# Two feed-forward passes over eight experts: the lead between the two products, and which engine rectifies which tile

## The chip, the cores and the metric

The kernel runs on one NeuronCore of one Trainium2 chip. The metric is the device time of one execution in microseconds (us). TensorE (PE) multiplies and transposes, ScalarE (ACT) and VectorE (DVE) read PSUM and write SBUF, GpSimd (POOL) issues the indirect DMAs, SyncE (SP) the direct ones. Each engine runs its own queue in order and waits on semaphores.

## The reference, cut to what matters

```python
def _L0_ffn_ref(tgt, Wr, br, W1, b1, W2, b2, gamma, beta):
    logits = jnp.einsum('bsd,ed->bse', tgt, Wr) + br
    top_v, top_i = jax.lax.top_k(logits, 2)
    ...
    h = jax.nn.relu(jnp.einsum('bsd,efd->bsef', tgt, W1) + b1)
    o = jnp.einsum('bsef,edf->bsed', h, W2) + b2
    tgt2 = jnp.einsum('bsed,bse->bsd', o, router_w)
    return _layer_norm(tgt + tgt2, gamma, beta)
x = x + 0.5 * _L0_ffn_ref(_layernorm(x), ...)
x = x + _L0_attn_ref(_layernorm(x), ...)
x = x + 0.5 * _L0_ffn_ref(_layernorm(x), ...)
```

There are 4 batches of 1024 rows, D = 128, F = 512, 8 experts, two experts to a row, all in float32. The attention is a difference of two softmaxes; the change does not touch it.

## The kernel before

**Stages.** Setup and first routing take up to about 51 us, the first expert pass 51 to 210 us, attention over four batches 210 to 450 us, the second expert pass 450 to 622 us, and the merge of the last two batches the rest.

**An expert pass** works on tiles of 128 routed rows, all of one expert. There are two groups (two batches each) of GSLOTS = 39 tiles, so SLOTS = 78 tiles to a pass; T counts tiles over both passes. For tile T, PE transposes the gathered rows into bank 0 (`turn_x`, L1059). ACT copies the result to SBUF (`copy_xT`, L692) and copies the expert's first weight, 128x512, to a staging buffer (`stage_w1`, L698). PE makes the first product in four blocks of 128 hidden units (`first`, L1066), which the profile shows as 8 records. ACT rectifies blocks 0 and 1 (`relu_first`, L705), DVE blocks 2 and 3 (`relu_rest`, L1579). PE accumulates the second product over the four blocks (`second`, L1076, again 8 records), and DVE adds the bias b2 and stores the tile in a ring of 16 (`add_b2`, L1587). The first product of a tile lies in two PSUM banks, two blocks in each, and two tiles alternate in banks 2 to 5. The y tiles alternate in banks 6 and 1. `xT`, `w1s` and `hT` have two buffers each, cut from `scratch` by `lent`.

**The order is written out by hand.** Each engine has its own `step(p, s)`. On PE, step s is `turn_x(s+2)`, `first(s+1)`, `second(s)`. On ACT it is `copy_xT(s+2)`, `stage_w1(s+2)`, `relu_first(s+1)`. On DVE it is `add_b2(s-1)`, `relu_rest(s+1)`. The loops run from s = -2. `turn_x(T)` waits for `xT_sb >= T`, that is, until ACT has copied tile T-1 out of bank 0. `second(T)` also waits for `add_b2(T-2)`. `expert_offset` loads the register with the place of tile s+2's expert on each engine.

**Side work sits between steps.** In pass one DVE carries the routing of the second group (s = 0 to 18) and, from s = 49, the merge of batch 0 in pieces (`MERGING`, `first_merge`); its 13th piece, at s = 61, is `batch_stats` (L1332). In pass two DVE does `last_route` in steps 0 to 3, whose fourth piece is again `batch_stats`. ACT makes rows in two halves of four normalisations (L644) at s = 5 and 6 of pass two and rescales sums in the same manner at s = 66, 67, 75 and 76.

**POOL** works one list in order. In pass one it gathers the rows of each tile (`gather_x`, L486, one indirect DMA), five up front and later as far as the transposes allow. After tile 55 it mixes these with gathers of results (L507); `rstd(BATCHES)`, which waits for the statistics of s = 61, stands just ahead of `gather_x(68)`, and tiles 68 to 77 follow. In pass two the rows are loaded by SP (`load`, L383), and POOL writes every finished tile to `results` (`send`, L518). Its list there is: three scatters (L494), `rstd(n)` (waits for the fourth piece of `last_route`), three scatters, then 78 sends; one scatter follows each of the first ten, and two follow each of sends 16 to 23. `rstd` stands again after sends 63 and 72. SP loads tile T into its ring slot only when send T-16 has landed, and tile 39, the first of the second group, only when all scatters have landed (`group_ready(1)`).

The change touches `hT_at`, `hT_of`, `staged`, `xT_of`, `copy_xT`, `stage_w1`, `relu_first`, `relu_rest`, `first`, `second`, the three `step` functions and the loop starts.

Of the kernel before, what the change touches and what calls it, by code (L numbers as in the profile page):

```python
# [14 lines left out]
P = 128  # L15
# [15 lines left out]
def macaron_kernel(nc, x_in, w_q12, w_k12, w_v, lq1, lk1, lq2, lk2, Wr, br, W1, b1, W2, b2, gamma, beta, out):  # L31
    BATCHES, S, D = x_in.shape
    E, F, _ = W1.shape
# [26 lines left out]
    with ctx:  # L60
# [91 lines left out]
        xt, xT, w1s, hT, ys = lent(RING * ROW), lent(2 * P), lent(2 * F), lent(2 * F), lent(RING * D)  # L152
        assert at[0] <= ATT
# [5 lines left out]
        def lent_z(n):  # L159
# [9 lines left out]
        assert at[0] <= ATT  # L169
# [14 lines left out]
         xT_ps, xT_sb, hT_ps, hT_sb, y_ps, y_sb,  # L184
# [7 lines left out]
            "hT_ps", "hT_sb", "y_ps", "y_sb", "z_used", "xn_ready",  # L192
# [12 lines left out]
        hT_first = sem("hT_first")  # L205
# [29 lines left out]
        def xT_of(T):  # L235

            return xT[:, T % 2 * P:(T % 2 + 1) * P]

        def staged(T, c, n=1):

            return w1s[:, T % 2 * F + c * P:T % 2 * F + (c + n) * P]

        def hT_at(T, c):

            return bank(2 + 2 * (T % 2) + 2 * c // FC, c % (FC // 2) * P, (c % (FC // 2) + 1) * P)

        def hT_of(T, c):

            return hT[:, (T % 2 * FC + c) * P:(T % 2 * FC + c + 1) * P]
# [47 lines left out]
        Y_BEHIND, Y_NEAR = 12, 7  # L297
        BETA_AT = 18
# [322 lines left out]
        def _(act):  # L621
# [66 lines left out]
            def copy_xT(T):  # L688
                act.wait_ge(xT_ps, T + 1)
                if T >= 2:  # L690
                    act.wait_ge(hT_ps, 2 * T - 2)
                act.activation(xT_of(T), bank(0, 0, P), ACT.Copy).then_inc(xT_sb, 1)  # L692

            def stage_w1(T, at):

                if T >= 2:
                    act.wait_ge(hT_ps, 2 * T - 2)
                act.activation(staged(T, 0, FC), blocks[:, bass.ds(at, F)], ACT.Copy).then_inc(w1_sb, 1)  # L698

            def relu_first(T, at):  # L700
                act.wait_ge(hT_ps, 2 * T + 1)
                if T >= 2:
# [3 lines left out]
                ins.then_inc(hT_first, 1)  # L706
# [186 lines left out]
            for s in range(-2, SLOTS):  # L893
# [3 lines left out]
                if s == GSLOTS - 3:  # L897
# [14 lines left out]
            for s in range(-2, SLOTS):  # L912
# [10 lines left out]
                if s == GSLOTS - 3:  # L923
# [27 lines left out]
        def _(pe):  # L951
# [109 lines left out]
            def first(T):  # L1061
# [180 lines left out]
            for s in range(-2, SLOTS):  # L1242
                if s == GSLOTS - 2:
# [13 lines left out]
            for s in range(-2, SLOTS):  # L1257
                if s in (TURN_AT, TURN_AT + 1):
                    turn_rows(a, s - TURN_AT)
                if s == GSLOTS - 2:  # L1260
# [34 lines left out]
        def _(dve):  # L1295
# [278 lines left out]
            def relu_rest(T, at):  # L1574
                dve.wait_ge(hT_ps, 2 * T + 2)
                if T >= 2:
                    dve.wait_ge(y_ps, T - 1)
                for c in range(FC // 2, FC):
                    ins = dve.tensor_scalar(hT_of(T, c), hT_at(T, c), blocks[:, B1_AT + c:][:, bass.ds(at, 1)], 0.0, ALU.add, ALU.max)  # L1579
                ins.then_inc(hT_sb, 1)  # L1580
# [10 lines left out]
            def step(p, s):  # L1591
# [349 lines left out]
            for s in range(-2, SLOTS + 1):  # L1941
# [33 lines left out]
            for s in range(-2, SLOTS + 1):  # L1975
# [59 lines left out]
```

## Time and profile before

| what | value |
|---|---|
| device time, median of 3 runs | 656.39 us (655.84 to 657.74) |
| the profiled execution: time, span | 657.03 us, 655.3 us |
| PE busy | 586.6 us, 90% of the span |
| DVE, ACT, POOL busy | 452.0, 441.4, 388.8 us |
| first product, L1066, 1248 records | 171.2 us busy, mean 281 ns |
| second product, L1076, 1248 records | 167.1 us busy, mean 277 ns |
| mean granted TensorE clock | 0.954 |

A matmul record shows 275 ns but the next one starts about 0.11 us later: they overlap, and the pace is read from starts. The timeline merges equal instructions in a row ("x8") and gives the idle time of the engine before them with what ended it in square brackets. A granted clock of 1.00 is 2.4 GHz, 0.50 is 1.2 GHz.

### The profile page before, as it was taken

How to read it: one execution, taken by the hardware profiler on the slowest of the kernel's cores; microseconds unless marked ns; L12 is line 12 of the kernel's file. 1: busy time of each engine (PE TensorE's matmuls, PEld its weight loads, DVE VectorE, ACT ScalarE, POOL GpSimd, SP SyncE). 2: the span in 40 equal slices, each digit the busy share in tenths (PEclk: the TensorE clock that was granted, in tenths of full speed). 3: DMA queues.
4: the chain of work that ended last, by engine and by line, in shares of the span. 5: the costliest groups of instructions: out<-in, count | busy, mean ns of one | idle time of the engine just before them, and what ended most of it. 6: DMA issues, size and time to landing. Idle time of an engine off the chain costs nothing.

```text
span 655.3 us, 16513 instructions
## 1 busy us (share of the span) xinstructions
PE 586.6 (90%) x4362; PEld 538.8 (82%) x4362; DVE 452.0 (69%) x1421; ACT 441.4 (67%) x1146; POOL 388.8 (59%) x481
## 2 busy tenths in 40 slices
PE   5987999999998888899898999798999959999945
PEld 5877999999998677787796888687999959998911
DVE  4775788446685989699689868956567534477635
ACT  4755666676667586768885975775876636877724
POOL 3006565657577785587424575784577777655623
PEclk9587999999999999899999999997999998999968
DMA  8902223223234110000000000112233323621051
GB/s 249 313 23 58 78 74 75 79 77 88 74 72 84 44 30 9 18 24 26 2 1 2 12 30 25 42 44 57 65 75 88 104 66 84 210 79 40 29 192 65
DMA packets 41881, 45.96 MB, mean 70 GB/s; under 512 B 8726, under 2 KB 32706, under 8 KB 41536
## 3 DMA queue, kind: packets, MB, share of 16 engines
q1 hardware_dynamic: 32496, 27.13, 14.2%
q0 software_dynamic: 9088, 17.75, 9.8%
q8 instruction: 39, 0.64, 0.4%
q14 instruction: 50, 0.41, 0.2%
q10 hardware_dynamic: 208, 0.02, 0.0%
HBM read 25.95 MB, written 19.83 MB: 70 GB/s over the span
## 4 chain that ended last, share of the span: by engine, by line
PE 47%; DVE 21%; POOL 10%; issue 9%; ACT 8%; DMA 3%; DVEq 0%; ACTq 0%; SPq 0%; POOLq 0%
PE banks L1066 16%; PE banks L1076 15%; DVE nb L1829 6%; DVE scratch L1836 3%; POOL rows L494 3%; POOL results L518 2%; PE banks L1163 2%; PE banks L1059 2%; PE banks L954 2%; PE banks L956 2%; PE banks L955 2%; DVE st_r L1326 1%; POOL rs L475 1%; ACT scratch L780 1%; POOL zb L507 1%
## 5 line engine op out<-in xcount | busy, mean ns | idle before, releaser
L1066 PE MATMUL banks<-scratch 128*128 128x128 f32 x1248 | 171.2, 281 | 1.5 <-ACT scratch L698 0.9
L1076 PE MATMUL banks<-blocks,scratch 128*128 x1248 | 167.1, 277 | 2.4 <-ACT scratch L705 1.3
L1579 DVE TENSOR_SCALAR scratch<-banks,blocks 128x128 f32<-128x128 f32 x312 | 95.0, 345 | 98.4 <-PE banks L1066 88.0
L1066 PEld LDWEIGHTS banks<-scratch 128*128 128x128 f32 x1248 | 156.3, 197 | 5.0 <-issue 4.5
L1076 PEld LDWEIGHTS banks<-blocks,scratch 128*128 128x128 f32 x1248 | 152.7, 193 | 4.5 <-issue 4.0
L486 POOL DMA_INDIRECT scratch<-xrows,rowbuf x78 | 75.2, 964 | 82.7 <-DVE rowbuf L1474 41.8
L692 ACT ACTIVATE scratch<-banks 128x128 f32<-128x128 f32 x156 | 43.2, 277 | 102.8 <-PE banks L1059 99.2
L780 ACT ACTIVATE scratch<-banks,nb 128x1024 f32<-128x1024 f32 x64 | 71.4, 1116 | 47.5 <-DVE nb L1829 47.1
L518 POOL DMA_INDIRECT results<-scratch x78 | 79.2, 1015 | 37.7 <-issue 20.1
L705 ACT ACTIVATE scratch<-banks,blocks 128x128 f32<-128x128 f32 x312 | 96.8, 365 | 2.5 <-PE banks L1066 2.0
L698 ACT ACTIVATE scratch<-blocks 128x512 f32 x156 | 97.2, 623 | 0.3
L1829 DVE TENSOR_REDUCE nb<-banks 128x1 f32<-128x1024 f32 x64 | 76.3, 1215 | 10.4 <-PE banks L956 9.5
L494 POOL DMA_INDIRECT rows<-rowbuf,slot x64 | 68.4, 1068 | 22.6 <-issue 16.2
L1163 PE MATMUL banks<-xn,scratch 128*128 128x128 f32 x512 | 64.8, 281 | 1.6 <-ACT scratch L766 1.6
L954 PE MATMUL banks<-xnTh,xmh 128*128 128x512 f32 x128 | 53.3, 417 | 14.1 <-ACT scratch L780 13.6
L1163 PEld LDWEIGHTS banks<-xn,scratch 128*128 128x128 f32 x512 | 61.7, 197 | 3.0 <-issue 2.0
L1587 DVE TENSOR_TENSOR scratch<-banks,blocks 128x128 f32<-128x128 f32 x156 | 44.9, 288 | 27.2 <-PE banks L1076 19.7
L507 POOL DMA_INDIRECT zb<-yrows,slot x48 | 50.4, 1050 | 15.3 <-issue 12.5
L1059 PE MATMUL banks<-ident,scratch 128*128 128x128 f32 x156 | 44.3, 284 | 11.9 <-issue 4.7
L956 PE MATMUL banks<-xnTh,xml 128*128 128x512 f32 x128 | 50.3, 393 | 0.0
L955 PE MATMUL banks<-xnTl,xmh 128*128 128x512 f32 x128 | 50.0, 391 | 0.0
L1836 DVE SCALAR_TENSOR_TENSOR scratch<-scratch,cc 128x1024 f32<-128x1024 f32 x32 | 40.9, 1279 | 5.7 <-POOL cc L566 5.7
(264 smaller groups left out, 879.5 us busy)
## 6 DMA issues: line engine op xcount, KB each, us to landing
scratch<-rows SPq DMA_DIRECT2D x78, 64.5 KB, 2.0
yrows<-scratch SPq DMA_DIRECT2D x78, 64.0 KB
scratch<-in_L_ffn_W_dram SPq DMA_DIRECT2D x1, 2048.0 KB, 21.2
xrows<-tgt SPq DMA_DIRECT2D x4, 512.0 KB, 4.0
x<-in_L_attn_x_dram SPq DMA_DIRECT2D x3, 512.0 KB, 8.5
scratch<-xrows,rowbuf POOLq DMA_INDIRECT x78
results<-scratch POOLq DMA_INDIRECT x78
rows<-padrows SPq DMA_DIRECT2D x18, 64.5 KB
```

Of the source, the lines that this page charges most:

```text
L486: pool.indirect_dma_start(xt_v[:, r, 0:D], None, xrows, bass.IndirectOffsetOnAxis(idx[:, T:T + 1], 0)).then_inc(came_or_sent[r], 16)
L494: pool.indirect_dma_start(rows[b // GB], bass.IndirectOffsetOnAxis(slot_v[:, b, j, k:k + 1], 0), rows_of(b)[:, j, k, :], None).then_inc(ro ...
L518: pool.indirect_dma_start(results, bass.IndirectOffsetOnAxis(xt_v[:, r, D:ROW].bitcast(I32), 0), ys[:, r * D:(r + 1) * D], None, bounds_ch ...
L698: act.activation(staged(T, 0, FC), blocks[:, bass.ds(at, F)], ACT.Copy).then_inc(w1_sb, 1)
L705: ins = act.activation(hT_of(T, c), hT_at(T, c), ACT.Relu, bias=blocks[:, B1_AT + c:][:, bass.ds(at, 1)], scale=1.0)
L780: act.activation(pp, banks[:, 2 * m * 512:(2 * m + 2) * 512], ACT.Exp, bias=nb[:, 2 * i + m:2 * i + m + 1], scale=1.0, accum_out=ll[:, i:i ...
L954: pe.matmul(o, ah, bh, start=True, stop=False)
L1066: ins = pe.matmul(hT_at(T, c), staged(T, c), xT_of(T), start=True, stop=True)
L1076: ins = pe.matmul(y_at(T), hT_of(T, c), blocks[:, W2_AT + c * D:][:, bass.ds(at, D)], start=(c == 0), stop=(c == FC - 1))
L1163: ins = pe.matmul(bank(6, 0, D), dT[t % 2][:, k * P:(k + 1) * P], vb[:, k * D:(k + 1) * D], start=(k == 0), stop=(k == TB - 1))
L1579: ins = dve.tensor_scalar(hT_of(T, c), hT_at(T, c), blocks[:, B1_AT + c:][:, bass.ds(at, 1)], 0.0, ALU.add, ALU.max)
L1829: dve.tensor_reduce(nb[:, c], banks[:, 2 * m * 512:(2 * m + 2) * 512], AX_X, ALU.max, negate=True).then_inc(nb_ready, 1)
```

## The change

The lead of the first product over the second grows from one tile to two (`H_LEAD = 2`), that of the transpose from two tiles to four (`X_LEAD = 4`). The first product of a tile lies in one PSUM bank, and four tiles rotate through banks 2 to 5. An even tile is rectified whole by ACT, an odd one whole by DVE. `xT`, `w1s` and `hT` get a third buffer. On PE the first product comes ahead of the transpose in a step, and the loops begin at s = -4 on PE and ACT and s = -3 on DVE. The two waits of `second` for the rectified tile become one.

```diff
-        xt, xT, w1s, hT, ys = lent(RING * ROW), lent(2 * P), lent(2 * F), lent(2 * F), lent(RING * D)
-        assert at[0] <= ATT
+        xt, xT, w1s, hT, ys = lent(RING * ROW), lent(3 * P), lent(3 * F), lent(3 * F), lent(RING * D)
+        assert at[0] <= ATT + S
...
         def hT_at(T, c):
 
-            return bank(2 + 2 * (T % 2) + 2 * c // FC, c % (FC // 2) * P, (c % (FC // 2) + 1) * P)
+            return bank(2 + T % 4, c * P, (c + 1) * P)
...
+        H_LEAD, X_LEAD = 2, 4
+        assert H_LEAD % 2 == 0 and SLOTS % 2 == 0
...
             def copy_xT(T):
                 act.wait_ge(xT_ps, T + 1)
-                if T >= 2:
-                    act.wait_ge(hT_ps, 2 * T - 2)
+                if T >= 3:
+                    act.wait_ge(hT_ps, T - 2)
...
-            def relu_first(T, at):
-                act.wait_ge(hT_ps, 2 * T + 1)
-                if T >= 2:
-                    act.wait_ge(y_ps, T - 1)
-                for c in range(FC // 2):
+            def relu_even(T, at):
+                act.wait_ge(hT_ps, T + 1)
+                if T >= 3:
+                    act.wait_ge(y_ps, T - 2)
+                for c in range(FC):
...
-                if s + 2 < SLOTS:
-                    e_at[s + 2] = expert_offset(ACTE, s + 2)
-                    copy_xT(t + 2)
-                    stage_w1(t + 2, e_at[s + 2])
-                if 0 <= s + 1 < SLOTS:
-                    relu_first(t + 1, e_at.pop(s + 1))
+                if s + X_LEAD < SLOTS:
+                    e_at[s + X_LEAD] = expert_offset(ACTE, s + X_LEAD)
+                    copy_xT(t + X_LEAD)
+                    stage_w1(t + X_LEAD, e_at[s + X_LEAD])
+                at = e_at.pop(s + H_LEAD, None)
+                if 0 <= s + H_LEAD < SLOTS and s % 2 == 0:
+                    relu_even(t + H_LEAD, at)
...
                 for c in range(FC):
                     ins = pe.matmul(hT_at(T, c), staged(T, c), xT_of(T), start=True, stop=True)
-                    if (c + 1) % (FC // 2) == 0:
-                        ins.then_inc(hT_ps, 1)
+                ins.then_inc(hT_ps, 1)
 
             def second(T, at):
-                pe.wait_ge(hT_first, T + 1)
-                pe.wait_ge(hT_sb, T + 1)
+                pe.wait_ge((hT_even, hT_odd)[T % 2], T // 2 + 1)
...
-                if s + 2 < SLOTS:
-                    turn_x(t + 2)
-                    w_at[s + 2] = expert_offset(PE, s + 2)
-                if 0 <= s + 1 < SLOTS:
-                    first(t + 1)
+                if 0 <= s + H_LEAD < SLOTS:
+                    w_at[s + H_LEAD] = expert_offset(PE, s + H_LEAD)
+                    first(t + H_LEAD)
+                if s + X_LEAD < SLOTS:
+                    turn_x(t + X_LEAD)
                 if s >= 0:
                     second(t, w_at.pop(s))
...
-                if s + 2 < SLOTS:
-                    e_at[s + 2] = expert_offset(DVE, s + 2)
-                if 0 <= s + 1 < SLOTS:
-                    relu_rest(t + 1, e_at[s + 1])
+                if s + H_LEAD + 1 < SLOTS:
+                    e_at[s + H_LEAD + 1] = expert_offset(DVE, s + H_LEAD + 1)
+                if 0 <= s + H_LEAD < SLOTS and s % 2 == 1:
+                    relu_odd(t + H_LEAD, e_at[s + H_LEAD])
```

## Rows read from the trace of the kernel before

**Rows 1.** Timeline of PE, pass one, steady: two transposes one step apart

```profile
121.09 0.27 PE L1059 MATMUL banks<-ident,scratch 128*128 128x128 f32 x1
122.98 0.27 PE L1059 MATMUL banks<-ident,scratch 128*128 128x128 f32 x1
```

**Rows 2.** Timeline of PE: transposes of tiles 3 and 77 of pass one, its end

```profile
57.39 0.27 PE L1059 MATMUL banks<-ident,scratch 128*128 128x128 f32 x1
...
204.50 0.27 PE L1059 MATMUL banks<-ident,scratch 128*128 128x128 f32 x1
...
209.87 0.60 PE L1105 MATMUL banks<-ident,xn 128*128 128x128 f32 x4
```

**Rows 3.** Instructions of line L1019 (`find_ids`) in pass one: duration min/median/max in ns

```profile
L1019 PE MATMUL banks<-rowbuf,zb x32: 195/198/202, 95.8 to 103.7; 128*128 128x78 bf16 x32
```

**Rows 4.** Timeline of POOL and PE: gathers 0, 68, 69, their `rstd`; transposes 0, 66

```profile
48.36 1.21 POOL L486 DMA_INDIRECT scratch<-xrows,rowbuf  x1 [41.78 <-DVE rowbuf L1474]
...
51.30 0.45 PE L1059 MATMUL banks<-ident,scratch 128*128 128x128 f32 x1 [3.85 <-DMA scratch<-xrows,rowbuf]
...
179.77 0.27 POOL L474 TENSOR_SCALAR rs<-mv 128x8 f32<-128x8 f32 x1 [5.20 <-DVE mv L1332]
...
182.10 0.27 PE L1059 MATMUL banks<-ident,scratch 128*128 128x128 f32 x1
...
182.90 1.10 POOL L486 DMA_INDIRECT scratch<-xrows,rowbuf  x1 [0.52 <-PE banks L1059]
184.31 0.95 POOL L486 DMA_INDIRECT scratch<-xrows,rowbuf  x1 [0.30 <-PE banks L1059]
```

**Rows 5.** Timeline of PE around two idle times, and a window's busy times and clock

```profile
259.14 1.95 PE L1163 MATMUL banks<-xn,scratch 128*128 128x128 f32 x16
263.75 1.22 PE L1096 MATMUL banks<-ident,xn 128*128 128x128 f32 x8 [2.65 <-ACT scratch L757]
265.27 3.29 PE L1163 MATMUL banks<-xn,scratch 128*128 128x128 f32 x16 [0.30 <-ACT scratch L766]
...
447.20 0.43 PE L1048 MATMUL banks<-cnt,upper 128*128 128x64 f32 x2 [2.27 <-DVE cnt L1505]
...
449.00:450.00 1.00, 1.00 (x7) 1.00 (x6) 0.86 (x5) 0.00 (x0) 0.00 (x0) 0.50 0.26 62
```

**Rows 6.** Timeline of POOL and PE in pass two: POOL's list starts, last scatter, tile 39

```profile
463.49 0.26 POOL L474 TENSOR_SCALAR rs<-mv 128x8 f32<-128x8 f32 x1 [6.79 <-DVE mv L1332]
...
533.70 0.96 POOL L494 DMA_INDIRECT rows<-rowbuf,slot  x1 [0.30 <-issue]
...
539.10 0.45 PE L1059 MATMUL banks<-ident,scratch 128*128 128x128 f32 x1 [4.68 <-issue]
```

**Rows 7.** Timeline of ACT at the rescaling of s = 66 and 67

```profile
601.35 0.26 ACT L692 ACTIVATE scratch<-banks 128x128 f32<-128x128 f32 x1
601.51 0.62 ACT L698 ACTIVATE scratch<-blocks 128x512 f32 x1
602.03 0.61 ACT L705 ACTIVATE scratch<-banks,blocks 128x128 f32<-128x128 f32 x2
602.53 1.64 ACT L644 ACTIVATE sum_r<-sum_r,nm,rs 128x128 f32<-128x128 f32 x4
```

**Rows 8.** Timeline of PE: transposes 41 and 77 of pass two, its last second product

```profile
545.65 0.27 PE L1059 MATMUL banks<-ident,scratch 128*128 128x128 f32 x1
...
616.38 0.27 PE L1059 MATMUL banks<-ident,scratch 128*128 128x128 f32 x1
...
620.74 1.15 PE L1076 MATMUL banks<-blocks,scratch 128*128 x8 [0.52 <-ACT scratch L705]
```

**Rows 9.** Timeline of DVE and POOL: statistics ahead of `add_b2(72)`, sends 72 and 77

```profile
613.15 0.63 DVE L1332 BATCH_NORM_AGGREGATE mv<-st_r 128x2 f32<-128x6 f32 x8
...
614.81 0.97 POOL L518 DMA_INDIRECT results<-scratch  x1 [0.63 <-issue]
...
624.25 1.22 POOL L518 DMA_INDIRECT results<-scratch  x1 [0.30 <-issue]
```

More of the change, by code:

```diff
@@ L168, in macaron_kernel @@
         cmp2 = lent_z(GSLOTS * E)
-        assert at[0] <= ATT
+        assert at[0] <= ATT + S
         eidf, offf, roff = lent_z(GSLOTS), lent_z(GSLOTS), lent_z(GSLOTS)
@@ L183, in macaron_kernel @@
          gap_ready, gap_exp, cnt_ready, prefix_ps, slots_ready, table_ready, pads_sent,
-         xT_ps, xT_sb, hT_ps, hT_sb, y_ps, y_sb,
+         xT_ps, xT_sb, hT_ps, hT_odd, y_ps, y_sb,
          z_used, xn_ready, xnT_ps, xnTh_sb, xnTl_sb, qkT_ps, qkT_sb, M_ps, M_sb, xm_ps, xmh_sb, xml_sb,
@@ L204, in macaron_kernel @@
         last_done = sem("last_done")
-        hT_first = sem("hT_first")
+        hT_even = sem("hT_even")
         x_loaded = [sem(f"x_loaded{b}") for b in range(BATCHES)]
@@ L235, in xT_of @@
         def xT_of(T):
-            return xT[:, T % 2 * P:(T % 2 + 1) * P]
+            return xT[:, T % 3 * P:(T % 3 + 1) * P]
         def staged(T, c, n=1):
-            return w1s[:, T % 2 * F + c * P:T % 2 * F + (c + n) * P]
+            return w1s[:, T % 3 * F + c * P:T % 3 * F + (c + n) * P]
         def hT_at(T, c):
-            return bank(2 + 2 * (T % 2) + 2 * c // FC, c % (FC // 2) * P, (c % (FC // 2) + 1) * P)
+            return bank(2 + T % 4, c * P, (c + 1) * P)
         def hT_of(T, c):
-            return hT[:, (T % 2 * FC + c) * P:(T % 2 * FC + c + 1) * P]
+            return hT[:, (T % 3 * FC + c) * P:(T % 3 * FC + c + 1) * P]
         def y_at(T):
@@ L892, in _ @@
             act.wait_ge(table_ready, 1)
-            for s in range(-2, SLOTS):
+            for s in range(-X_LEAD, SLOTS):
                 step(0, s)
@@ L896, in _ @@
                     pair_gap(1)
-                if s == GSLOTS - 3:
+                if s == GSLOTS - X_LEAD - 1:
                     act.wait_ge(table_ready, 2)
@@ L911, in _ @@
             b, a = BATCHES - 1, 2 * BATCHES - 1
-            for s in range(-2, SLOTS):
+            for s in range(-X_LEAD, SLOTS):
                 step(1, s)
@@ L922, in _ @@
                     gap(a)
-                if s == GSLOTS - 3:
+                if s == GSLOTS - X_LEAD - 1:
                     act.wait_ge(table_ready, 4)
@@ L1241, in _ @@
             pe.wait_ge(table_ready, 1)
-            for s in range(-2, SLOTS):
-                if s == GSLOTS - 2:
+            for s in range(-X_LEAD, SLOTS):
+                if s == GSLOTS - H_LEAD:
                     pe.wait_ge(table_ready, 2)
@@ L1256, in _ @@
             pe.wait_ge(table_ready, 3)
-            for s in range(-2, SLOTS):
+            for s in range(-X_LEAD, SLOTS):
                 if s in (TURN_AT, TURN_AT + 1):
                     turn_rows(a, s - TURN_AT)
-                if s == GSLOTS - 2:
+                if s == GSLOTS - H_LEAD:
                     pe.wait_ge(table_ready, 4)
@@ L1572, in table, with relu_odd @@
                 yield
[L1574 to L1578, printed above, removed]
+            def relu_odd(T, at):
+                dve.wait_ge(hT_ps, T + 1)
+                if T >= 3:
+                    dve.wait_ge(y_ps, T - 2)
+                for c in range(FC):
                     ins = dve.tensor_scalar(hT_of(T, c), hT_at(T, c), blocks[:, B1_AT + c:][:, bass.ds(at, 1)], 0.0, ALU.add, ALU.max)
-                ins.then_inc(hT_sb, 1)
+                ins.then_inc(hT_odd, 1)
             def add_b2(T, at):
@@ L1940, in _ @@
             lows_1 = pair_lows()
-            for s in range(-2, SLOTS + 1):
+            for s in range(-H_LEAD - 1, SLOTS + 1):
                 step(0, s)
@@ L1974, in _ @@
             adding = [last_add(b) for b in range(GB)]
-            for s in range(-2, SLOTS + 1):
+            for s in range(-H_LEAD - 1, SLOTS + 1):
                 step(1, s)
```

8 lines of the change are left out of this document (4 added, 4 removed).

## The prediction

> **What bounds the kernel now.** I read the page's busy times first: PE is at work for 90% of the span, so a change to the expert passes pays only where PE waits in them. Next comes the PE timeline of a quiet stretch. From transpose to transpose a step is 1.89 us [rows 1] for 1 + 8 + 8 = 17 records; over longer stretches it is 1.897 us, or 0.1116 us a record and 0.89 us for a product. The attention's blocks of 16 records have that same spacing (1.95 us, less 0.275 of the last, over 15, is 0.112) [rows 5]. So a quiet step is PE's own pace. The change adds and removes no matmul, and a longer lead can win nothing there. What it can win are the waits between quiet stretches; what it can lose is where data arrive late. I summed both, pass by pass, from the starts of the transposes.
>
> **Pass one: what it removes.** From the transpose of tile 3 to that of tile 77 there are 74 steps in 147.1 us [rows 2]; 74 x 1.897 is 140.4, so 6.7 us are over. Work between the steps takes some of that: 32 records of L1019 [rows 3] at about 0.04 us spacing (1.2 us) and 8 other records (0.9). That leaves 4.6 us of waits. From tile 77 to the transposes behind the last second product are 5.4 us [rows 2] for 41 records (4.6): 0.8 more. Of these 5.4 us about 1.3 lie around the three later blocks of `find_ids`, where PE waits for DVE's comparison tiles and then refills its queue; the lead does not touch that wait. The other 4.1 us are waits for a rectified tile or for ACT. Now such a tile has from the end of `first(T)` to `second(T)` one second product and one step, 1.9 us, less 0.6 for two blocks. Then it has 3.8 us, less 1.2 for four. I count -4.0 us. The ends are -5.3 (the 1.3 go too) and -2 (half comes back as waits for the transposed copy, below).
>
> The one bank for a tile costs at most 0.45 us more from product to rectified tile, since ACT cannot begin at half of it; the cover is the 2.5 us just named, and without it each tile would pay that. The Trainium skill speaks for the same delay ("PSUM — Partial Sum Buffer", PSUM bank collisions raise a hardware error): two engines must stay out of one bank together, so four blocks in one bank cannot be rectified while the fourth is being made. By that alone the change would look worse than the old halves; with the lead the sum is the same either way.
>
> **Pass one: what it adds.** The transpose of tile T now stands at step T-4 instead of T-2, and the gathers must be there. At the start they are: POOL needs 1.25 us a gather, PE nearly 2 us a tile at the low clock. But `gather_x(68)` sits on POOL behind `rstd`, which waits 5.20 us for the statistics of s = 61 [rows 4], and that wait is tied to DVE's step, not to the lead. Before, POOL reads them at 179.77, issues tile 68 at 182.90, and a gather lands 2.9 us after its issue begins (48.36 to 51.30) [rows 4]: 185.8, just in time for its transpose at 185.9. On the same scale the new DVE runs these statistics 0.3 us earlier (step 60 has no rectifying; step 61 has all four blocks but starts them one transpose earlier), so tile 68 lands at about 185.4. PE begins step 64 at 182.10 [rows 4], makes `first(66)` until 183.0 and then stands at `turn_x(68)`, with `second(64)` queued behind it: a stall of 2.3 us, and 0.3 to refill. Ends: 0 (POOL early) and 3.3. Tile 69, 1.4 us behind on POOL [rows 4], comes in time, and so do the rest.
>
> A stall of that size has a second price. PE waited 2.27 us at 447.20, and the granted clock was 0.50 soon after; it waited 2.65 us at 263.75, and then 16 records took 3.29 us where 1.95 is usual [rows 5]: with the 8 records ahead of them, 1.5 us lost. Shorter idle times had no such sequel that I saw. I take 1.5 us; the ends are 0 and 3.
>
> The page "TensorE: Matmul & The Clock Gate" of the Trainium skill, Part 1, says that a lack of activity lowers the clock from 2.4 to 1.2 GHz and activity brings it back, and in HAM oscillation that waits for DMA between short bursts do this. By that rule the gather stall would cost more than its length, as the rows say too.
>
> Pass one: -4.0 + 2.3 + 0.3 + 1.5 = +0.1 us. The attention moves with its end; POOL, whose gathers reach into it, is earlier by more, so it holds nothing up. I credit nothing for that (0 to -1).
>
> **Pass two up to tile 39.** Nothing PE saves here counts, as POOL's list sets the arrival of tile 39. From 463.49 to the last scatter at 533.70 POOL works without a pause at 1.27 us an instruction, and PE gets tile 39 at 539.10 after 4.68 us of idleness [rows 6]. That list starts with `rstd`, which waits for DVE's statistics of step 3. In the new order `first(5)` instead of `first(4)` precedes them (one product and two transposes more, +1.1 us), and DVE rectifies four blocks ahead of them instead of two (+0.6), but step 2 rectifies nothing (-0.6). So POOL starts 1.05 us later, and tile 39 comes 1.05 us later. Ends: +0.5 and +1.7. Tiles 34 to 38 make PE wait as well, since it asks for them two steps earlier; that is inside the same wait.
>
> **Pass two behind tile 39.** When PE stands at `turn_x(39)` it has run second products up to 34 instead of 36. By the end of `second(72)` it has two seconds, one first (74) and two transposes more to do than before: 3 x 0.89 + 0.22 = 2.9 us. It saves waits. From tile 41 to tile 77 are 70.7 us for 36 steps (68.3) [rows 8], 2.4 us over: 0.6 at one place and 1.9 at the rescaling of s = 66 and 67. There ACT is the limit, and partly stays it. A copy is followed by the next instruction after 0.16 us, staging takes 0.52, two rectified blocks 0.50, four normalisations 1.54 [rows 7]; the new even step is 0.17 + 0.52 + 1.03 + 1.55 = 3.3 us, the odd one 2.2. Bank 0 is still the only place for a transpose, so `turn_x` may find the copy at most about 1.2 us late. Two steps have 5.5 us of work in 3.8: 0.5 us of the 1.9 stay. Saved: 0.6 + 1.4 = 2.0. So `second(72)` ends 1.05 + 2.9 - 2.0 = 1.95 us later.
>
> **The tail.** From send 72 on POOL has `rstd` and five sends back to back, 9.44 us from 614.81 to 624.25 [rows 9], and the end follows send 77. Send 72 waits for `add_b2(72)`, which before stood behind eight aggregates on DVE (613.15) [rows 9], 0.9 us late; now step 72 has no rectifying, and it is not late. So send 77, and the end, come 1.95 - 0.9 = 1.05 us later. The wait of 0.52 us for the last second product [rows 8] goes, but POOL covers it: worth nothing.
>
> **Sum.** +0.1 + 1.05 = +1.15 us on the profiled execution (657.03 us, span 655.3), which lies 0.64 above the median. On the median of 656.39 that gives 657.5 us.
>
> **Rivals.** *Tile 68 arrives in time (faster).* If DVE's statistics or POOL come 2.3 us earlier against PE, the stall and its clock go: -4.0 + 1.05 = -2.95, 653.4 us. For it: DVE is relieved in every other step. Against it: POOL's 5.20 us of waiting hang on one numbered step.
>
> *The stall stays, the clock does not fall.* 2.27 us is the shortest idle time with a sequel [rows 5]. -1.4 + 1.05 gives 656.0 us.
>
> *ACT's long even step blocks the transposes (slower).* The copy out of bank 0 now queues behind four rectified blocks and any side work. It decides from a lateness of 1.2 us: even step plus normalisations is 3.3 us against a step of 1.9, which is 1.4 late. Then the 1.4 us at the rescaling aren't won, the last 0.8 us of pass one neither, and the eight steps with weighing add 0.2: +1.15 + 2.4 is +3.6, 660.0 us. For it: the single bank 0. Against it: the odd step gives back what the even one takes.
>
> *The lead does nothing.* The removed waits return under other names, and the stalls are covered: 656.4 us.
>
> **How the numbers follow.** The forecast, stall with low clock, gets 0.35, the first rival 0.2, the second 0.2, the third 0.2, the last 0.05. The range runs from 652.5 (the first rival, with the 1.3 us partly won) to 661.5 (the third, with POOL's start at +1.7 and a longer low clock). A measurement of this kernel can tell about 0.3%, 2 us, from no change. Faster by more than that: most of the first rival and some of the spread of the others, 0.27. Slower: the third rival and the upper third of the forecast, 0.32. Within: 0.41.
>
> **What would show it.** In the new trace: quiet steps still 1.89 us; no PE wait for L705 or DVE in the middle of a pass; before the transpose of tile 68 of pass one some 2.3 us of idleness ended by the gather, with a granted clock of 0.50 behind it; POOL's `rstd` in pass two one microsecond later relative to the start of the pass; tile 39 of pass two also 1 us later; sends 72 to 77 still back to back. The prediction is wrong if quiet steps change their pace, if tile 68 is there, or if PE waits for L692 in many steps.

## The result, and the profile after

The changed kernel takes 661.59 us (median of 4, 660.02 to 662.77), the kernel before 656.49 beside it: ratio 1.0079, 95% interval 1.0052 to 1.0106, so about 5 us slower. The forecast was 657.5 with a range to 661.5: the sign of its sum was right, its size was a quarter of what was measured, and the result lies just outside the range.

The profiled execution took 660.02 us, span 658.3. The page of the changed kernel, its span and busy times:

```profile
span 658.3 us, 16355 instructions
PE 580.5 (88%) x4362; PEld 535.5 (81%) x4362; DVE 446.7 (68%) x1421; ACT 439.3 (67%) x1146; POOL 389.7 (59%) x481
```

PE, DVE and ACT are each busy for less time than before (586.6, 452.0 and 441.4 us), with the same count of instructions, while the span is 3 us longer. So the loss is not more work; it is waiting, and a low clock behind some of the waits. The quiet step is unchanged (timeline of PE, pass one, against [rows 1]; columns: start, duration, engine, line, operation, out<-in, shapes, count, and in brackets the idle time before it with its releaser):

```profile
119.36 0.27 PE L1062 MATMUL banks<-ident,scratch 128*128 128x128 f32 x1
...
121.26 0.27 PE L1062 MATMUL banks<-ident,scratch 128*128 128x128 f32 x1
```

1.90 us, as before. In the middle of pass one PE waits for neither ACT nor DVE by more than 0.25 us. In pass two it waits 1.06 us at 472.6 and 1.61 us at 476.8 for tables that ACT makes (line L1036); the wait for tile 39 behind them covers both. The time lies in a few other places, which the table gives stage by stage. Each stage runs between two instructions that every kernel here has; "T" is a transpose, "list" POOL's `rstd` that opens its list in pass two. The last two columns are experiments told below: the gather edit together with the routing edit, put on the kernel before and on the changed one.

| stage, us | before | after | before + edits | after + edits |
|---|---|---|---|---|
| start to T 0 of pass one | 51.3 | 49.7 | 52.3 | 50.9 |
| to the attention's first product | 160.7 | 162.0 | 160.0 | 157.1 |
| to T 0 of pass two | 238.5 | 238.9 | 238.8 | 238.3 |
| to POOL's list | 13.0 | 14.4 | 10.6 | 11.8 |
| to T 39 | 75.6 | 75.0 | 75.2 | 75.7 |
| to send 72 | 75.7 | 77.3 | 75.6 | 76.0 |
| to send 77 | 9.4 | 9.8 | 9.5 | 9.8 |
| to the end of the span | 31.0 | 31.2 | 31.0 | 30.9 |
| span | 655.3 | 658.3 | 653.0 | 650.5 |

The first line is chance: gather 0 waits for DVE's routing, which the change does not touch, and came 1.6 us earlier in this execution of after (the eight profiles taken where the kernel before takes 656 us have 49.6 to 52.3 there). Without it the stages add up to +4.6 us. A second profile of each kernel, taken one beside the other, has 51.5 and 51.3 us there, and spans of 655.7 and 660.4: +4.7.

**Pass one.** Timelines of POOL, then PE, of the changed kernel around tile 68 (against [rows 4]), and three windows of 2 us with PE's granted clock (the figure behind the five engines' busy times):

```profile
176.94 0.35 POOL L476 TENSOR_SCALAR rs<-mv 128x8 f32<-128x8 f32 x1 [4.35 <-DVE mv L1333]
...
180.15 1.26 POOL L488 DMA_INDIRECT scratch<-xrows,rowbuf  x1 [0.52 <-issue]
```

```profile
179.41 1.06 PE L1069 MATMUL banks<-scratch 128*128 128x128 f32 x8
183.11 0.33 PE L1062 MATMUL banks<-ident,scratch 128*128 128x128 f32 x1 [2.65 <-DMA scratch<-xrows,rowbuf]
...
184.80 1.91 PE L1069 MATMUL banks<-scratch 128*128 128x128 f32 x8
186.50 0.42 PE L1062 MATMUL banks<-ident,scratch 128*128 128x128 f32 x1
```

```profile
180.00:182.00 2.00, 0.47 (x5) 0.28 (x3) 1.74 (x7) 0.00 (x0) 1.54 (x2) 1.00 0.10 29
183.50:185.50 2.00, 2.00 (x12) 2.00 (x12) 0.29 (x1) 1.81 (x6) 1.49 (x2) 0.56 0.22 64
185.50:187.50 2.00, 2.00 (x13) 2.00 (x13) 0.64 (x3) 0.54 (x2) 1.59 (x2) 0.58 0.35 96
```

`gather_x(68)` starts 3.2 us behind `rstd` and lands 2.96 us later; PE stands for 2.65 us. The granted clock then falls from 1.00 to 0.56, near the 1.2 GHz level; a product of 8 records, 0.89 us at the full clock, stretches to 1.70 (184.80 to 186.50). From `first(66)` (179.41) to the transpose of tile 69 (186.50) are 7.1 us where 2.8 are usual, and 0.3 more go behind it: 4.6 us lost at one place, 2.65 of it the wait and most of the rest, 1.8 us, the low clock. "TensorE: Matmul & The Clock Gate" of the Trainium skill (Part 1) says that idleness brings the clock down and work brings it up again; the last two windows agree, and the price here is those 1.8 us.

The end of pass one, timelines of DVE, then PE:

```profile
206.43 1.12 DVE L1580 TENSOR_SCALAR scratch<-banks,blocks 128x128 f32<-128x128 f32 x4 [1.04 <-PE banks L1069]
207.47 0.68 DVE L1803 TENSOR_TENSOR xnTl<-banks,xnTh 128x512 fp32r<-128x512 f32 x1
208.07 0.48 DVE L1588 TENSOR_TENSOR scratch<-banks,blocks 128x128 f32<-128x128 f32 x2
```

```profile
208.59 1.15 PE L1077 MATMUL banks<-blocks,scratch 128*128 x8 [0.53 <-DVE scratch L1588]
```

The last second product waits for a free result bank. `add_b2`, which frees it, stands behind the four blocks of the last odd tile and a side piece of 0.6 us. The kernel before waited for ACT at this place (timeline of PE):

```profile
208.88 1.15 PE L1076 MATMUL banks<-blocks,scratch 128*128 x8 [0.25 <-ACT scratch L705]
```

These 0.25 us had a shorter wait ahead of them and a refill behind. From `second(75)` to the transposes behind the last second product, PE takes 0.79 us more than its records need at 0.1116 us each, in the kernel before and in the changed one alike (with the two edits told below it is 0.33 on the kernel before and again 0.79 on the changed one). The waits there changed their cause and not their sum.

**Pass two.** Timelines of DVE, POOL and PE of the changed kernel (against [rows 6]): the statistics ahead of the list, its start, its last scatter, tile 39.

```profile
463.10 1.12 DVE L1580 TENSOR_SCALAR scratch<-banks,blocks 128x128 f32<-128x128 f32 x4 [0.30 <-PE banks L1069]
464.14 0.63 DVE L1333 BATCH_NORM_AGGREGATE mv<-st_x 128x2 f32<-128x6 f32 x8
```

```profile
464.98 0.27 POOL L476 TENSOR_SCALAR rs<-mv 128x8 f32<-128x8 f32 x1 [8.68 <-DVE mv L1333]
...
534.80 0.96 POOL L496 DMA_INDIRECT rows<-rowbuf,slot  x1 [0.30 <-issue]
```

```profile
540.00 0.47 PE L1062 MATMUL banks<-ident,scratch 128*128 128x128 f32 x1 [4.37 <-DMA scratch<-rows]
```

The list starts 1.5 us later on the clock of the trace, 1.4 us later against T 0; tile 39 comes 0.8 us later against T 0.

**The tail.** Timelines of DVE and POOL of the changed kernel (against [rows 9]):

```profile
612.43 1.11 DVE L1580 TENSOR_SCALAR scratch<-banks,blocks 128x128 f32<-128x128 f32 x4
613.47 0.68 DVE L1789 TENSOR_TENSOR x<-x,sum_r 128x512 f32<-128x512 f32 x1
614.06 0.47 DVE L1327 BATCH_NORM_STATS2 st_r<-xn 128x6 f32<-128x128 f32 x2
614.86 0.29 DVE L1588 TENSOR_TENSOR scratch<-banks,blocks 128x128 f32<-128x128 f32 x1 [0.32 <-PE banks L1077]
615.23 0.64 DVE L1333 BATCH_NORM_AGGREGATE mv<-st_r 128x2 f32<-128x6 f32 x8
615.79 0.26 DVE L1588 TENSOR_TENSOR scratch<-banks,blocks 128x128 f32<-128x128 f32 x1
```

```profile
616.00 0.97 POOL L520 DMA_INDIRECT results<-scratch  x1 [1.01 <-DVE scratch L1588]
617.28 0.97 POOL L520 DMA_INDIRECT results<-scratch  x1 [0.31 <-issue]
...
627.09 1.02 POOL L520 DMA_INDIRECT results<-scratch  x1 [0.30 <-issue]
```

DVE works without a gap from 612.43 to 614.5. So `add_b2(71)` (614.86) comes 2.15 us after the end of `second(71)`, where it was 1.38 us in the kernel before with the same side work; `add_b2(72)` (615.79) comes 1.18 us after the end of `second(72)`, and send 72 cannot start before send 71 is off. (The end of a product is taken here and below as the start of PE's next record, 614.61 for `second(72)`.)

### The profile page after: what moved, and what is told of

It reads as the page before. It is cut to its first block, busy times and chain, and to the rows that moved or that the text cites. A ratio compares the mean times of both kernels' runs of the same rounds, so it can differ in the third digit from the quotient of the medians.

```text
span 658.3 us, 16355 instructions
## 1 busy us (share of the span) xinstructions
PE 580.5 (88%) x4362; PEld 535.5 (81%) x4362; DVE 446.7 (68%) x1421; ACT 439.3 (67%) x1146; POOL 389.7 (59%) x481
## 4 chain that ended last, share of the span: by engine, by line
PE 54%; DVE 21%; POOL 9%; issue 7%; ACT 5%; DMA 3%; DVEq 0%; SPq 0%; ACTq 0%; POOLq 0%
PE banks L1069 19%; PE banks L1077 18%; DVE nb L1830 5%; DVE scratch L1837 3%; PE banks L1062 3%; PE banks L1164 3%; PE banks L957 2%; PE banks L959 2%; PE banks L958 2%; POOL rows L496 2%; POOL zb L509 1%; DVE zb L1466 1%; DVE st_r L1327 1%; POOL scratch L509 1%; ACT tgt L646 1%
## 5 line engine op out<-in xcount | busy, mean ns | idle before, releaser
L1580 DVE TENSOR_SCALAR scratch<-banks,blocks 128x128 f32<-128x128 f32 x312 | 88.2, 344 | 52.8 <-PE banks L1069 49.4
L488 POOL DMA_INDIRECT scratch<-xrows,rowbuf x78 | 76.9, 986 | 75.7 <-DVE rowbuf L1475 40.1
L707 ACT ACTIVATE scratch<-banks,blocks 128x128 f32<-128x128 f32 x312 | 88.6, 373 | 1.1 <-PE banks L1069 1.1
L509 POOL DMA_INDIRECT zb<-yrows,slot x48 | 49.6, 1034 | 18.8 <-issue 12.5
```

The source lines that it names most:

```text
L488: pool.indirect_dma_start(xt_v[:, r, 0:D], None, xrows, bass.IndirectOffsetOnAxis(idx[:, T:T + 1], 0)).then_inc(came_or_sent[r], 16)
```

## The experiments

Most of these kernels are the kernel before or the changed kernel with one or more of three edits. The **gather edit** (POOL) takes four more gathers, tiles 68 to 71, ahead of the statistics in pass one:

```diff
-            for T in range(ahead + 4, ahead + 8):
+            for T in range(ahead + 4, ahead + 12):
                 gather_x(T)
             rstd(BATCHES)
-            for T in range(ahead + 8, SLOTS):
+            gather(1, range(1, 2))
+            for T in range(ahead + 12, SLOTS):
                 gather_x(T)
-                if T in (ahead + 11, ahead + 14):
-                    gather(1, range((T - ahead - 8) // 3, (T - ahead - 8) // 3 + 1))
+                if T == ahead + 14:
+                    gather(1, range(2, 3))
```

The **routing edit** (DVE) takes the last statistics two pieces a step, so they are done in steps 0 and 1 of pass two instead of 0 to 3:

```diff
                 if s >= STATS_AT:
                     next(routing, None)
+                    next(routing, None)
```

The **add edit** (DVE) moves the last additions of one batch four steps later, so that step 71 loses its piece of 0.6 us:

```diff
-                    if LAST_AT + 20 + LAST_BY * f <= s < LAST_AT + 24 + LAST_BY * f:
+                    if LAST_AT + 24 + LAST_BY * f - 4 * f <= s < LAST_AT + 28 + LAST_BY * f - 4 * f:
                         next(adding[f], None)
```

The gather edit acts in pass one alone and the other two in pass two alone, so the trace of a kernel with several still shows what each does.

**Control: both kernels once more.**

> The changed kernel itself once more, as the control for the experiments: they ran where the kernel before takes 766 us instead of 656, with ACT and DVE standing still for 4 to 22 us at a time (released by nothing the profile names) while POOL issues gathers or scatters back to back. Theory (tile 68 arrives late, then the low clock; add_b2 late behind the four-block odd step): after stands above before here too, by 0 to +6 us, and its transpose of tile 68 waits for DMA; a kernel without the late gather then lies 3 to 5 us under it beyond what the same move gives the kernel before (8 us). Rival (ACT's long even step): the loss shows as PE waiting for ACT in quiet steps, also here, over +6 us.

> The kernel before, profiled where it takes 766 us: it shows the long standstills of ACT and DVE without the change. If they belong to the place and not to the change, they lie at the same POOL bursts (155 to 188 us and 530 to 620 us), sum to about 100 us, and quiet steps are still 1.89 us apart.

Measured: 661.9 us (4 runs) against 656.3 (14 runs), ratio 1.0082 (1.0054 to 1.0111). Tile 68 is waited for again, 2.71 us. The standstills that the expectations speak of were absent from both profiles, so the second expectation found nothing to measure; they are told in the last section. The loss repeats, and the late gather with it.

**Both edits on the changed kernel, and on the kernel before.**

> The changed kernel with four gathers ahead of POOL's statistics and the last routing work two pieces a step, the match to the kernel before with the same edits (652.96). Theory: pass one is 158.2 us from its first transpose to the attention (162.0 in the changed kernel), POOL's list starts 2.8 us earlier after the first transpose of pass two (11.6 instead of 14.4), and in the tail the adds are late by about 1 us as in the changed kernel: 653.5 us. If the third edit of a_tail is worth nothing, 652.2. Rival (the two edits hide each other): 655 us or more. Where engines stand still, as in seven earlier runs, about 760.

> The kernel before with four gathers ahead of the statistics and the last routing work taken two pieces a step. Theory: the gather move alone gave 8 us here; two pieces a step takes nothing from the path, so 757 to 759 us. If the routing pieces hold up the adds behind them, 755.

Measured: on the changed kernel 652.58 us (10 runs), ratio to before 0.9954 (0.9938 to 0.997), which is 9 us under the changed kernel's time (8 by the ratios; it was not run beside them). The expectation was 653.5. On the kernel before 652.96 (9 runs), ratio 0.995 (0.9933 to 0.9967). The second expectation, 757 to 759, was made for a place where the kernel before takes 766 us, and fell together with that place.

Timelines of POOL, then PE, of the changed kernel with both edits (its lines stand one further down):

```profile
178.37 0.27 POOL L476 TENSOR_SCALAR rs<-mv 128x8 f32<-128x8 f32 x1
```

```profile
181.24 0.27 PE L1063 MATMUL banks<-ident,scratch 128*128 128x128 f32 x1
...
183.14 0.27 PE L1063 MATMUL banks<-ident,scratch 128*128 128x128 f32 x1
```

POOL's `rstd` finds its input ready, tile 68 (181.24) is transposed without a wait, and the step stays 1.90 us: no low clock. Pass one takes 157.1 us instead of 162.0 (158.1 in the kernel with three edits, below). The same edit gives the kernel before 0.7 us (160.7 to 160.0), so 3 to 4 us of the changed kernel's time were the late gather and its low clock, and they belong to the change. This is the disputed step of pass one, shown.

In pass two the list starts 2.6 us earlier against T 0 (14.4 to 11.8) and tile 39 comes 1.9 us earlier; on the kernel before it is 2.4 us (13.0 to 10.6) and 2.7. That gain has nothing to do with the change, but the change's own price can be read across: 1.2 us at the list with the edit, 1.4 without; 1.7 us at tile 39 with it, 0.8 without. A third part is a surprise: from T 39 to send 72 are 76.0 us instead of 77.3. Timeline of PE behind tile 39, first of the changed kernel, then with both edits:

```profile
540.26 2.01 PE L1077 MATMUL banks<-blocks,scratch 128*128 x8
542.07 1.91 PE L1069 MATMUL banks<-scratch 128*128 128x128 f32 x8
543.77 0.42 PE L1062 MATMUL banks<-ident,scratch 128*128 128x128 f32 x1
543.99 1.81 PE L1077 MATMUL banks<-blocks,scratch 128*128 x8
```

```profile
534.11 2.00 PE L1078 MATMUL banks<-blocks,scratch 128*128 x8
535.90 1.47 PE L1070 MATMUL banks<-scratch 128*128 128x128 f32 x8
537.21 0.27 PE L1063 MATMUL banks<-ident,scratch 128*128 128x128 f32 x1
537.32 1.06 PE L1078 MATMUL banks<-blocks,scratch 128*128 x8
```

The low clock lasts for a product and a half instead of three: 1.3 us. A third kernel (below) has the same work there and lost 0.8 us more than this one, so at least most of the 1.3 us is spread between executions and not the edit's.

What this pair settles: with the two late arrivals mended in both, the kernels are equal (652.6 and 653.0). By stages the change then gives 2.9 us in pass one and pays 1.2 at the list, 0.5 up to T 39, 0.5 up to send 72 and 0.4 in the burst of sends.

**All three edits.**

> The changed kernel with four gathers ahead of the statistics, the last routing work two pieces a step, and the first half's last addition on DVE four steps later. Theory (the four-block odd step with side work makes add_b2 of tiles 71 and 72 late): send 72 follows second(72) by 1.5 us or less instead of 2.7, and the end comes about 1 us earlier than without the third edit, 755 us. Rival (sends are bound by POOL alone): no change, 756 us.

Measured: 652.23 us (6 runs), ratio 0.9934 (0.9914 to 0.9955), which overlaps that of the two edits: no gain at the end. But the adds did move. `add_b2(71)` now comes 1.15 us after `second(71)`, where it was 2.16 with two edits, and send 72 starts 2.03 us after the end of `second(72)` instead of 2.69; the expectation was 1.5 or less. Timeline of DVE:

```profile
607.27 0.29 DVE L1589 TENSOR_TENSOR scratch<-banks,blocks 128x128 f32<-128x128 f32 x1 [0.32 <-DVE st_r L1328]
607.64 0.69 DVE L1637 TENSOR_TENSOR sum_r<-sum_r,gammab 128x512 f32<-128x512 f32 x1
608.37 0.65 DVE L1334 BATCH_NORM_AGGREGATE mv<-st_r 128x2 f32<-128x6 f32 x8
608.93 0.26 DVE L1589 TENSOR_TENSOR scratch<-banks,blocks 128x128 f32<-128x128 f32 x1
```

The first piece that the edit moved (L1637, 0.6 us) landed right ahead of the aggregates and of `add_b2(72)` (608.93), so only part of the lateness went. And what went did not reach the end. From T 39 to the end of `second(72)` PE took 0.8 us more than in its twin, the kernel with two edits, at the low clock behind T 39, and the burst of sends took 10.5 us instead of 9.8: sends 73, 75 and 76 last 1.47, 1.14 and 1.46 us where the twin has 1.11, 0.97 and 1.32. In all eight profiles taken where the kernel before takes 656 us each send of over 1.2 us ran beside a 128x512 operation of DVE, though not each send beside one was long; that the one causes the other was not tested.

So it is shown that side work in step 71 makes `add_b2(71)` and send 72 late. The share of the four blocks themselves rests on the rows of the tail above: no kernel that takes them out of the odd step was run. In pass one this kernel took 158.1 us where its twin took 157.1; by the transpose of tile 10 it was already 1.0 us behind, at the low clock of the start. So 1 us is the spread of a stage between executions.

**A lead of three for the transposes.**

```diff
-        H_LEAD, X_LEAD = 2, 4
+        H_LEAD, X_LEAD = 2, 3
```

> The changed kernel with transposes three steps ahead instead of four, nothing else. Theory: tile 68 is asked for 1.9 us later, so the wait of 2.65 us ahead of its transpose shrinks to about 0.8 and the low clock behind it goes: pass one 3 us shorter, POOL's list in pass two starts 1 us earlier, 657.5 us. Rival (ACT's copy and staging need the fourth step: the odd step brings them one step ahead of first(T) only): PE waits for ACT's staging in every second step, about 0.3 us each in 150 steps, 680 us or more, as it was where engines stood still (30 us above before).

Measured: 694.47 us (4 runs), ratio 1.0571 (1.0531 to 1.0612), 33 us above the changed kernel. Tile 68 is indeed not waited for, but the rival holds, and in every step instead of every second one. Timelines of PE and ACT in a quiet stretch:

```profile
118.19 0.27 PE L1062 MATMUL banks<-ident,scratch 128*128 128x128 f32 x1
118.30 1.06 PE L1077 MATMUL banks<-blocks,scratch 128*128 x8
119.44 1.13 PE L1069 MATMUL banks<-scratch 128*128 128x128 f32 x8
120.41 0.27 PE L1062 MATMUL banks<-ident,scratch 128*128 128x128 f32 x1
```

```profile
118.50 0.28 ACT L694 ACTIVATE scratch<-banks 128x128 f32<-128x128 f32 x1 [1.42 <-PE banks L1062]
118.67 0.62 ACT L700 ACTIVATE scratch<-blocks 128x512 f32 x1
```

From the transpose to the first product that uses it are 1.25 us (118.19 to 119.44): copy, then staging, then PE. PE has only one second product to put there, 1.00 us with the transpose. So every step is 2.21 us (118.30 to 120.52 in the same view) instead of 1.90, and the first products wait. Over some 150 steps that would be 47 us; a part is taken back where the waits for tiles 68 and 39 go. The order of the step explains it. Before, the transpose stood ahead of the first product of a step, and a lead of 2 left two products between; now it stands behind it, so a lead of 3 leaves one, and a lead of 4 leaves three. The longer reach for the gathers is thus the price of that order. A lead of three with the transpose ahead of the first product was not tried.

**The same edits where engines stood still.** Twelve runs, in five groups that each share their runs of the kernel before, fell at a place where that kernel takes 764 to 768 us. The changed kernel itself was not run there, so they tell little of the change. The first group of four, on the gather edit (on either kernel), the routing edit, and the lead of three:

> The changed kernel, with the gathers of tiles 68 to 71 moved ahead of the rstd on GpSimd that waits for the statistics of step 61. The theory (the loss of pass one is one late gather, a wait of 2.65 us and 1.7 us of low clock behind it) expects PE to find tile 68 in place, the clock to stay at 1.00 around 180 us, and the time to fall from 661.6 by about 4 us to 657.5, with everything behind pass one unchanged. The rival (the deeper lead and the four-block rectifying cost time throughout the passes, and the late gather is hidden by later waits) expects less than 1 us of gain.

> The kernel before with the same move on GpSimd. There tile 68 was just in time, so both theories expect no change: 656.5 us, within 1 us. A gain of several us here would say that the order of that list is a fault by itself and not one that the change meets.

> The changed kernel with two pieces of last_route to a step of VectorE in pass two, so that its statistics come in step 1 instead of step 3. The theory that GpSimd's list from its rstd to its last scatter sets the arrival of tile 39 expects that rstd, the last scatter and tile 39 all 3.5 us earlier and the whole time 3.5 us shorter, about 658 us. The rival (PE's own work up to tile 39 sets it) expects no change.

> The changed kernel with X_LEAD = 3: transposes three tiles ahead instead of four, the lead of the first product still two. The late-data theory expects the wait for tile 68 to shrink by one step, 2.65 to about 0.8 us, with no low clock behind it (-3.5 us), and one second product less to be left when PE stands at tile 39 of pass two (-0.9 us): about 657.2 us. The rival, that the cost lies in one bank to a tile and four blocks to an engine, expects no change from 661.6.

Two of them again elsewhere, and then the two edits together with a single run:

> The changed kernel, with the gathers of tiles 68 to 71 moved ahead of the rstd on GpSimd that waits for the statistics of step 61. The theory (the loss of pass one is one late gather, a wait of 2.65 us and 1.7 us of low clock behind it) expects PE to find tile 68 in place, the clock to stay at 1.00 there, and the time to be 4 us below that of the changed kernel, about 657.5 us where the kernel before takes 656.5, with everything behind pass one unchanged. The rival (deeper lead and four-block rectifying cost time throughout) expects less than 1 us of gain.

> The changed kernel with X_LEAD = 3. The late-data theory expects the wait for tile 68 to shrink from 2.65 to about 0.8 us, with no low clock behind it, and one second product less to be left at tile 39 of pass two: about 4 us below the changed kernel, 657 us where the kernel before takes 656.5. The rival, that the cost lies in one bank to a tile and four blocks to an engine, expects the time of the changed kernel, 661.5.

> The changed kernel with both orders mended: the gathers of tiles 68 to 71 ahead of the rstd of pass one, and two pieces of last_route to a step in pass two. If the two late arrivals are the loss, they add: about 4 us of the gather and 3.5 us of the earlier list in pass two, 654 us where the kernel before takes 656.5, with no wait of PE for tile 68 and tile 39 of pass two some 3.5 us earlier after the start of its pass than in the changed kernel (89.4 us). The rival (work per tile costs more) expects no change from the changed kernel.

A fourth group, meant for a place where the kernel before takes 656 us, and the gather edit once more at the end:

> The changed kernel with the gathers of tiles 68 to 71 ahead of POOL's statistics. Theory: the wait of 2.65 us ahead of the transpose of tile 68 and the low clock behind it go (4 us), the rest stays: 657.5 us, and the start of pass two is 4 us earlier. Rival (the stall was covered, and the loss is ACT's long even step): no earlier start of pass two, 661.

> The changed kernel with the last routing work two pieces a step, nothing else. Theory: the late gather of tile 68 stays, so pass one is as long as in the changed kernel; in pass two DVE reaches the statistics of step 3 sooner, POOL's list starts 2 to 3 us earlier, and tile 39 comes 2 us earlier: 659 us. Rival (tile 39 hangs on PE, not on POOL's list): 661.5 us.

> The changed kernel with both edits. Theory: 4 us and 2 to 3 us add up, since they lie in different passes: 654.5 us. The same two edits gave the kernel before 3.3 us (652.96), so the change would still stand 1 to 2 us above it, which is the late adds of the tail, and 652.2 with the third edit. If it comes out at 652.2 as well, the third edit is worth nothing.

> The changed kernel with transposes three steps ahead instead of four. Theory: tile 68's gather is asked for 1.9 us later, so its wait shrinks from 2.65 to below 0.8 us and the clock stays up; but the staged weights then are ready only one step ahead of first(T), so PE may wait for ACT. Without such a wait 658 us. Where engines stood still it took 30 us more than before, PE waiting 65 us for ACT's staging: if that belongs to the lead and not to the place, it comes back here, 680 us or more.

> The changed kernel with the gathers of tiles 68 to 71 ahead of POOL's statistics, nothing else. Theory: the wait for tile 68 and the low clock behind it go, pass one from its first transpose to the attention is 158.2 us instead of 162.0, and POOL's list in pass two starts 14.4 us after the first transpose of that pass, as in the changed kernel: 657.8 us. Rival (the routing edit shortens pass one too): pass one 160 us, 660 us.

None of the times expected for 656 us was met, as the base was another. What was measured, as ratios:

| edit | on | ratio to the kernel before, runs apart |
|---|---|---|
| gather | changed | 0.9929, 0.9917, 0.9899, 0.9938 |
| gather | before | 0.9896 |
| routing | changed | 0.9992, 0.9985 |
| both | changed | 0.9882, and 756.0 us against 766.8, one run each |
| lead of three | changed | 1.0407, 1.0386, 1.0434 |

On the changed kernel the gather edit is 5 us better there than the routing edit. But it gives the kernel before 8 us as well, where that has no late gather, so this says nothing of the late gather, and something else is in it: the edit moves POOL's gathers, and the standstills lie beside POOL's gathers. Alone, the gather edit was never run where the kernel takes 656 us; its share in the 9 us rests on the stage of pass one in the kernel with both edits, and that stage contains no other edit. The lead of three lies 31 to 32 us above the kernel before there, and 38 above it near 656 us.

## Why the prediction was wrong

Two steps failed. The tail was booked at -0.9 us and cost 0.85 (0.45 to send 72, 0.4 in the sends), since the sum left out what DVE's odd step 71 pushes ahead of the adds. And the 0.8 us behind tile 77 of pass one were booked as gain and stayed. The rest was right in its mechanism, with smaller errors in size. Step by step, each against the profile of after:

- *A quiet step is PE's own pace.* Right: 1.90 us, and nothing was won or lost there.
- *Pass one, what it removes: -4.0 us.* Right for the larger part, 3.2 us up to the place where tile 77 stood before, and wrong for the last 0.8. Counted over the same records, the waits between T 3 and `second(75)` shrink by 3.0 us (3.2 in the second pair of profiles), with the 4.6 us of the stall taken off. The step that failed is the last 0.8 us of the sum, the waits behind tile 77: there DVE has the four blocks of tile 77 and `xnTl` ahead of `add_b2`, PE waits for the bank, and the 0.79 us over the pace are all still there. The third rival named these 0.8 us, but put them down to ACT.
- *Pass one, what it adds: 2.3 + 0.3 + 1.5 = 4.1 us.* Right in place and cause, and near in size: 2.65 us of waiting, the clock at half, 4.6 us together (4.7 in the second profile). Part of that nearness is luck. Against T 0, PE came to `first(66)` 1.1 us earlier than the sum had it, since the waits saved ahead of it outweigh the longer lead's extra records; and POOL read the statistics 1.2 us earlier, where the sum had 0.3. The two errors nearly cancel. Removing the late gather returned 3.9 to 4.9. The rival *tile 68 arrives in time* was made true by an edit, and pass one then took 3.6 and 2.5 us less than before, where it said 4.0.
- *Pass one together: +0.1.* Measured +1.3 and +1.5.
- *Attention: 0.* Measured +0.4 in one pair of profiles and +1.0 in the other. The eight profiles taken where the kernel before takes 656 us lie between 238.3 and 239.7 without order; left open.
- *List of pass two +1.05, tile 39 +1.05.* Right: +1.4 and +0.8. DVE's four blocks stand ahead of the aggregates as said. The routing edit moved the list by 2.6 us and tile 39 by 1.9.
- *Behind tile 39, `second(72)` +0.9.* Right: from T 39 to its end 74.6 us instead of 73.5, +1.1 (+0.8 in the second pair). Most of the waits at the rescaling went, as forecast: of 2.5 us over the pace from step 64 to 72, 0.7 are left.
- *The tail: `add_b2(72)` not late, -0.9.* Wrong, the dearest step. The prediction looked at step 72 alone, which indeed has nothing to rectify. It did not look at the odd step before it: 1.1 us of rectifying, 0.6 of addition and 0.4 of statistics push `add_b2(71)` to 2.15 us behind its product, and the aggregates and `add_b2(72)` behind that. From the end of `second(72)` to send 72 are 2.67 us; they were 2.22. Forecast -0.9, measured +0.45, and the burst of sends takes 0.4 more (send 76 takes 1.32 us where 0.97 is usual, beside an addition of DVE, L1789). That DVE's work in step 71 sets send 72 is shown by the third edit; how much of the 0.45 us is the blocks is only read from the rows.

The terms that were off add up: 1.2 in pass one (0.8 at its end, 0.5 in the stall), 0.4 in the attention, -0.3 up to tile 39, 0.2 behind it, 1.35 at send 72, 0.4 in the burst, 0.15 at the end: 3.4 us, which is what lies between +1.15 and the stages' +4.6. Of the rivals, *the clock does not fall* and *the lead does nothing* are excluded by the rows. *ACT's long even step* gave the nearest number (660.0), but its mechanism is not there: no transpose waits for ACT in a quiet stretch, and the gain at the rescaling came. What was long was DVE's odd step, which the prediction weighed only at the list.

## What to carry to other kernels

Who gives one engine all the work of every other step has to follow what that step pushes into the next ones: its queue can be idle for a third of the span (DVE is busy for 68%) and two microseconds late where side work shares a step. A longer lead moves requests to earlier steps, but not the loads that other queues' waits hold back; look up each load that stands behind a wait before lengthening a lead. And count how many products lie between a transpose and its use in the written order, not the lead in steps: here one step of lead less left one product where there were three, and cost 33 us, while one late load cost 4.6.

## What the runs showed of the hardware

An idle time of 2.65 us took the granted clock from 1.00 to 0.56, and PE ran at about half speed for some 20 records behind it. How long that lasts differs between executions: behind a wait of 4.4 us it was three products and more in one kernel, and one and a half behind 5.1 us in another.

The same kernel took 656 us in some groups of runs and 764 to 768 in others. There ACT and DVE (and PE behind them) stood still for up to 27 us at a time, with no releaser that the profile knows ("remote"), while POOL issued its indirect DMAs on at 1.25 us each. Timelines of ACT and of POOL from the changed kernel with the gather edit, at that place:

```profile
159.17 0.62 ACT L701 ACTIVATE scratch<-blocks 128x512 f32 x1
184.99 0.28 ACT L695 ACTIVATE scratch<-banks 128x128 f32<-128x128 f32 x1 [25.19 <-remote]
```

```profile
178.12 0.94 POOL L488 DMA_INDIRECT scratch<-xrows,rowbuf  x1 [0.30 <-issue]
...
180.62 0.95 POOL L488 DMA_INDIRECT scratch<-xrows,rowbuf  x1 [0.30 <-issue]
```

In that execution ACT spent 121 us in 23 such waits; the kernels near 656 us show none. From 150 to 210 us the DMA queues of kind instruction moved 2 and 3 packets there, where the changed kernel at 656 us has 5 and 5. That is in line with engines that wait for their instructions, but it was not tested, and the cause stays open. What follows for method is firm: the kernels were comparable only with the kernel before run beside them, and an edit of POOL's order that is worth 0.7 us at one place was worth 8 at the other.
